# Self-attention lead-in of a four-block transformer kernel: how the second half of queries and keys, the high and low parts and the spreading transfers are ordered

## What is computed

```python
x_norm = modulate(_ln(x), shift_a, scale_a)
qkv = x_norm @ W_qkv + b_qkv
q, k, v = jnp.split(qkv, 3, axis=-1)
q = q.reshape(B, N, NH, hd).transpose(0, 2, 1, 3)    # NH = 16 heads of hd = 16, N = 1024
k = k.reshape(B, N, NH, hd).transpose(0, 2, 1, 3)
v = v.reshape(B, N, NH, hd).transpose(0, 2, 1, 3)
attn_w = jax.nn.softmax(jnp.einsum('bhqd,bhkd->bhqk', q, k) * scale, axis=-1)
attn_out = jnp.einsum('bhqk,bhkd->bqhd', attn_w, v)
```

## Time and profile before

| | |
|---|---|
| runs | 1668.72, 1672.08, 1673.46 us; median 1672.08 |
| profiled execution | 1674.23 us, its span 1672.4 us |
| busy share of the span | TensorE 91%, VectorE 63%, ScalarE 46%, GpSimd 23% |
| chain that ended last | TensorE 68%, VectorE 19%, issue 6%, ScalarE 5%, DMA 1%, GpSimd 1% |
| clock granted to TensorE | mean 0.968 of full speed |

### The profile page before, as it was taken

How to read it: one execution, slowest core, us unless ns; L and a number is a source line. 1 busy time by engine, 2 the same in 40 slices (tenths; PEclk the granted TensorE clock), 3 DMA queues, 4 the chain that set the end, 5 groups by cost and what they waited for, 6 DMA issues and landing times.

```text
span 1672.4 us, 26374 instructions
## 1 busy us (share of the span) xinstructions
PE 1528.8 (91%) x10485; PEld 927.8 (55%) x10485; DVE 1049.2 (63%) x2946; ACT 769.9 (46%) x1228; POOL 379.4 (23%) x419
## 2 busy tenths in 40 slices
PE   5899998999998999878998999899999899887898
PEld 3456574444354857556764666543444476655676
DVE  3564344999727445899457334399991744579953
ACT  1315421588853533325543533138886354333444
POOL 3510005343016000114133000344400701001320
PEclk9898999999999999999999999899999999999999
DMA  9400007221020000000130000542202000000000
GB/s 337 140 1 0 0 22 161 37 39 31 2 76 1 1 1 2 2 1 2 32 133 1 0 1 1 143 66 40 40 2 77 1 1 1 3 1 1 1 1 25
DMA packets 37551, 59.60 MB, mean 36 GB/s; under 512 B 7360, under 2 KB 26980, under 8 KB 36532
## 3 DMA queue, kind: packets, MB, share of 16 engines
q1 hardware_dynamic: 25239, 34.71, 6.3%
q0 software_dynamic: 9408, 15.85, 6.1%
q10 hardware_dynamic: 2780, 7.36, 1.2%
HBM read 42.03 MB, written 2.10 MB: 26 GB/s over the span
## 4 chain that ended last, share of the span: by engine, by line
PE 68%; DVE 19%; issue 6%; ACT 5%; DMA 1%; POOL 1%; ACTq 0%; DVEq 0%; POOLq 0%
PE ps L993 9%; PE ps L1005 8%; PE ps L464 7%; PE ps L1299 4%; PE ps L978 3%; PE ps L870 3%; PE ps L1092 3%; DVE taken L2351 3%; PE ps L1100 3%; DVE rs L2036 2%; PE ps L848 2%; PE ps L592 2%; DVE mxw L2028 2%; PE ps L600 2%; PE ps L1156 2%
## 5 line engine op out<-in xcount | busy, mean ns | idle before, releaser
L2221 DVE TENSOR_REDUCE mm<-ps 128x1 f32<-128x1024 f32 x256 | 310.2, 1223 | 32.9 <-PE ps L978 25.6
L1618 ACT ACTIVATE pt<-ps 128x512 f32<-128x512 f32 x512 | 276.8, 599 | 59.1 <-PE ps L993 41.3
L2464 POOL TENSOR_TENSOR rstd<-ve,minus_half 128x4 f32<-128x4 f32 x32 | 35.7, 1116 | 748.8 <-DVE ve L1900 748.8
L993 PE MATMUL ps<-qx,kx 64*128 64x512 f32 x512 | 188.3, 445 | 1.0 <-ACT pt L1618 1.0
L978 PE MATMUL ps<-kx,qx 48*128 48x512 f32 x512 | 186.6, 444 | 0.2
L1005 PE MATMUL ps<-pt,v 128*32 128x256 f32 x2048 | 158.7, 390 | 0.0
L993 PEld LDWEIGHTS ps<-qx,kx 64*128 64x128 f32 x512 | 78.9, 184 | 95.9 <-ACT pt L1618 85.9
L2111 DVE TENSOR_TENSOR rlo<-ring,rhi 128x512 fp32r<-128x512 f32 x48 | 33.2, 692 | 114.5 <-ACT ring L1569 114.4
L1005 PEld LDWEIGHTS ps<-pt,v 128*32 128x32 f32 x2048 | 42.9, 108 | 85.6 <-ACT pt L1618 61.7
L978 PEld LDWEIGHTS ps<-kx,qx 48*128 48x128 f32 x512 | 75.4, 184 | 22.0 <-issue 18.0
L592 PE MATMUL ps<-filler 128*128 128x512 f32 x262 | 83.6, 434 | 0.0
(11 more groups left out here) (374 smaller groups left out, 3396.1 us busy)
## 6 DMA issues: line engine op xcount, KB each, us to landing
wm<-in_L_xcond_W_mlp_dram SPq DMA_DIRECT2D x4, 1024.0 KB, 7.9
qx<-q_hi POOLq DMA_DIRECT2D x64, 64.0 KB, 2.6
kx<-k_hi POOLq DMA_DIRECT2D x64, 64.0 KB, 2.8
w3a<-in_L_xcond_w_m_dram SPq DMA_DIRECT2D x2, 2048.0 KB, 8.1
w<-in_L_xcond_e_w_dram SPq DMA_DIRECT2D x6, 512.0 KB, 7.8
w<-in_L_xcond_e_w_dram SPq DMA_DIRECT2D x2, 1536.0 KB, 13.3
s_ada<-in_L_xcond_w_ada_dram ACTq DMA_DIRECT2D x1, 2304.0 KB, 23.0
qx<-q_lo POOLq DMA_DIRECT2D x32, 64.0 KB, 2.6
```

The source lines that it names most:

```text
L993: pe.matmul(ps[:, bank, :], kx[r, p % 4, kc * P:(kc + 1) * P], qx[r, p % 4, half * 512:(half + 1) * 512], start=True, stop=True).then_inc( ...
L1618: act.activation(pt[:, u % 8, half * 512:(half + 1) * 512], ps[:, bank, :], ACT.Exp, scale=QK_SCALE).then_inc(st_read, 1)
L2221: return dve.tensor_reduce(mm[:, p % 2, e, t:t + 1], place(), X, ALU.max).then_inc(ring_read, 1)
```

## The change

The matmuls of the second half are taken out of the lead-in. Six of its eight fp32 matmuls stand one by one behind the first six units of query scores (`full_step(m + 2)`), two before the loop. The gate rows are spread behind unit 8 instead of before the loop. The nine fillers before the loop and the fillers beside units 0 to 6 go; nine fillers are put ahead of the transposes of block 1 and four behind them; the fillers beside units 7 to 15 write bank 4. The first linear of block 1 waits for each chunk of `hT` by itself. High and low parts of chunk 0 are made for 512 tokens at a time: those of block 0 ahead of ScalarE's `ln(2, 1)`, those of block 1 behind it. `full_ready` is raised for q and k separately. `spread(0)` waits for each of q high, q low, k high and k low and sends each as soon as it is there; in every spread the four high transfers of q (or k) now come before its two low ones.

The core of the diff (left out: the removed `queries_keys` and `high_parts`, and semaphore counts that only follow):

```diff
 (TensorE)
-                linear(0, wqk2, 0, hT[:, 0])
+                linear(0, wqk2, 0, hT[:, 0]).then_inc(full_done, 1)
                 residual(1, 1)
                 pe.wait_ge(v_ready, b * NB + 1)
-                linear(2, wqk2, KC, hT[:, 0])
+                linear(2, wqk2, KC, hT[:, 0]).then_inc(full_done, 1)
+                keep_busy(6, 9)
                 ln(2, 1)
+                keep_busy(6, 4)
...
+                def full_step(j):
+
+                    qk, k, c = j // 4, j // 2 % 2, j % 2
+                    if j == 4:
+                        pe.wait_ge(v_ready, b * NB + NB)
+                    ins = pe.matmul(ps[:, 4 + 2 * qk + k, :], wqk2[:, c, (qk * KC + 1) * P:(qk * KC + 2) * P], hT[:, k, c, :], start=c == 0, stop=c == KC - 1)
+                    if j == 7:
+                        ins.then_inc(full_done, 1)
...
-                pe.wait_ge(hT_ready, b * 2 * N_HT + 12)
-                for qk in range(2):
-                    queries_keys(0, qk, take(), (1,)).then_inc(ring_ready, 1)
+                linear(take() + 1, wqk2, 0, hT[:, 1], (hT_ready, b * 2 * N_HT + 10)).then_inc(ring_ready, 1)
+                linear(take() + 1, wqk2, KC, hT[:, 1]).then_inc(ring_ready, 1)
                 values(1)
-                queries_keys(1, 0, 4)
-                pe.wait_ge(v_ready, b * NB + NB)
-                queries_keys(1, 1, 6).then_inc(full_done, 1)
+                full_step(0)
+                full_step(1)
                 pe.wait_ge(v2_clear, b + 1)
-                pe.wait_ge(ring_read, b * N_RING + 2)
-                keep_busy(2, 9)
-                pe.wait_ge(full_ready, b + 1)
-                for j in range(3):
...
-                    if n < 4:
-                        keep_busy(7, 2 if n < 0 else 1)
+                    if m == 7:
+                        pe.wait_ge(full_ready, b * 2 + 1)
+                    if 7 <= m and n < 4:
+                        keep_busy(4 if m < 2 * T else 7, 2 if n < 0 else 1)
...
+                    if m < 6:
+                        full_step(m + 2)
+                    elif m == 8:
+                        pe.wait_ge(full_ready, b * 2 + 2)
+                        for j in range(3):
...
 (ScalarE)
-                ln(2, 1, (mod, M_SC_A, M_SH_A))
...
+                def high_part(qk, k):
+
+                    col = (C_BQ2, C_BK2)[qk]
+                    affine(dense[2 * qk][:, k * BLK:(k + 1) * BLK], ps[:, 2 * qk + k, :], 1.0, colT[:, col:col + 1]).then_inc(hi_ready, 1)
+
+                for qk in range(2):
+                    act.wait_ge(full_done, b * 3 + qk + 1)
+                    high_part(qk, 0)
+                ln(2, 1, (mod, M_SC_A, M_SH_A))
...
                 for qk in range(2):
-                    high_parts(0, qk)
-                act.wait_ge(full_done, b + 1)
+                    act.wait_ge(ring_ready, u0 + qk + 1)
+                    high_part(qk, 1)
+                act.wait_ge(full_done, b * 3 + 3)
...
 (VectorE)
                 for qk in range(2):
-                    low_parts(qk)
+                    low_part(qk, 0)
+                for qk in range(2):
+                    place()
+                    low_part(qk, 1).then_inc(ring_read, 1)
                 add_v2(1)
...
 (GpSimd)
-                    if p == 0:
-                        pool.wait_ge(ring_read, b * N_RING + 2)
...
                     for qk, wide in enumerate((qx, kx)):
-                        for e in range(2):
-                            r = 32 * (p % 4) + HD * e
-                            for i, part in enumerate(((0, 1, 0), (0, 0, 1))[qk]):
-                                pool.dma_start(wide[64 * e + HD * i:64 * e + HD * (i + 1), p % 4, :], dense[2 * qk + part][r:r + HD, :]).then_inc(spread_ld[p % 4], 16)
+                        for part in range(2):
+                            if p == 0:
+                                if part == 0:
+                                    pool.wait_ge(hi_ready, b * 6 + 2 + qk + 1)
+                                else:
+                                    pool.wait_ge(ring_read, b * N_RING + qk + 1)
+                                pool.sem_inc(passed, 1)
+                            for e in range(2):
+                                r = 32 * (p % 4) + HD * e
+                                for i in range(3):
+                                    if ((0, 1, 0), (0, 0, 1))[qk][i] == part:
+                                        pool.dma_start(wide[64 * e + HD * i:64 * e + HD * (i + 1), p % 4, :], dense[2 * qk + part][r:r + HD, :]).then_inc(spread_ld[p % 4], 16)
```

More of the change, by code:

```diff
@@ L963, in take_key @@
                     return 4 + n % 3
-                def queries_keys(c, qk, bank, blocks=range(NB)):
-                    for k in blocks:
-                        ins = linear(bank + k, wqk2, qk * KC + c, hT[:, k])
-                    return ins
+                def full_step(j):
[5 more added lines that the diff above has]
+                        ins.then_inc(full_done, 1)
                 def query_scores(p, u):
@@ L1049, in _ @@
                         query_scores(q, at_m)
+                    if m < 6:
[3 more added lines that the diff above has]
+                        for j in range(3):
+                            o = N_ROW * b + R_G_A + j
+                            ins = pe.matmul(ps[:, 5 + j // 2, j % 2 * D:(j % 2 + 1) * D], row_of[:, o:o + 1].broadcast_to([64, P]), row_hl[:, :], start=True, stop=True)
+                        ins.then_inc(gates_spread, 1)
                     if n >= 0:
@@ L1626, in _ @@
                 for qk in range(2):
-                    high_parts(0, qk)
-                act.wait_ge(full_done, b + 1)
+                    act.wait_ge(ring_ready, u0 + qk + 1)
+                    high_part(qk, 1)
+                act.wait_ge(full_done, b * 3 + 3)
                 for qk in range(2):
                     col = (C_BQ2, C_BK2)[qk] + 1
-                    ins = affine(full[qk], ps[:, 4 + 2 * qk:6 + 2 * qk, :].rearrange("p a q -> p (a q)"), 1.0, colT[:, col:col + 1])
-                ins.then_inc(full_ready, 1)
+                    affine(full[qk], ps[:, 4 + 2 * qk:6 + 2 * qk, :].rearrange("p a q -> p (a q)"), 1.0, colT[:, col:col + 1]).then_inc(full_ready, 1)
                 act.wait_ge(gates_spread, b + 1)
@@ L1635, in _ @@
                 act.activation(gates[:, 2, :], ps[:, 6, 0:D], ACT.Copy).then_inc(gates_ready, 1)
-                act.wait_ge(full_ready, b + 1)
+                act.wait_ge(full_ready, b * 2 + 2)
                 for i in range(4):
@@ L1639, in _ @@
                 for qk in range(2):
-                    high_parts(1, qk)
+                    act.activation(dense[2 * qk][:, :], full[qk], ACT.Copy).then_inc(hi_ready, 1)
                 scored = 2
@@ L2211, in place, with low_part @@
                     return ps[:, 2 * (n % 2):2 * (n % 2) + 2, :].rearrange("p a q -> p (a q)")
[L2213 to L2217 removed]
+                def low_part(qk, k):
+                    dve.wait_ge(hi_ready, b * 6 + 2 * k + qk + 1)
+                    col, r = (C_BQ2, C_BK2)[qk], slice(k * BLK, (k + 1) * BLK)
+                    return dve.scalar_tensor_tensor(dense[2 * qk + 1][:, r], ps[:, 2 * qk + k, :], colT[:, col:col + 1], dense[2 * qk][:, r].bitcast(F32),
+                                                    ALU.add, ALU.subtract)
                 def query_maximum(p, u):
```

18 lines of the change are left out of this document (1 added, 17 removed).

## The result

The changed kernel takes 1716.12 us in the median of four runs (1713.93 to 1719.25), the kernel before 1672.12: the ratio is 1.0255, with a 95% interval of 1.0236 to 1.0275. It is 44 us slower where 12 us faster was forecast. The profiled execution took 1716.97 us, 42.7 more than that of before.

What follows compares the result with a forecast made beforehand. TensorE's chain and waits up to unit 0 were taken as the bound: 6.4 and 7.4 us gained in the batches, 13.8, less 1.8 for the clock, gives 12.0 and 1660.1 us; range 1655.5 to 1667.5.

Steps and rivals of the forecast that it cites:

- Fillers round the transposes: Around block 1's transposes: fillers keep the clock at 2.4 GHz, so k's linear ends 3.2 us earlier.
- Halves: Block 1's high parts made 512 columns at a time, 0.60 us each: q ready at 262.3, k at 264.1.
- piece by piece: Spread 0 on GpSimd: issues start at 262.95, after q's high part; all landed at 271.5 instead of 278.3.
- landings: Spread 0's transfers land 2.5 to 3.2 us after issue; 3.15 us taken.
- Rival C: Transfers come later because VectorE's work holds up GpSimd's issues: gains of only 5 to 9 us, 1663 to 1667; chance 0.13.
- The new wait ahead of unit 0: TensorE, after two full steps, has nothing to do for 2.9 us until the transfers land at 271.5.
- the sum of 13.8: Gain of both batches without any clock effect: 6.4 us in the first, 7.4 us in the second.
- The clock at unit 0: The new wait may drop the clock under units 0 to 5: 1.7 to 3.5 us lost, chance six in ten a batch.
- Rival E: Clock falls at unit 0 and stays low through the lead: 14.5 us more a batch, 15 us slower, 1687; chance 0.03.
- the lead lost: Units before unit 9 get denser with full steps: 2.4 us lost a batch, 3.1 if changes of shape cost extra.
- a limit of 1.223 us a unit: VectorE's reduction time for each unit of query scores; nine need 11.0 us, so it isn't the lead's bound.
- The cover of 0.35 us for ScalarE's copy of the maxima: Before the key scores: GpSimd's spreads move 6.75 us earlier, TensorE 6.4, so the copy is not late.

Runs made afterwards that it cites:

- e1_cover: The changed kernel with eleven fillers in the wait ahead of unit 0, also called the covered kernel: 1662.45 us median, ratio 0.9929.
- the burst: The changed kernel with 24 fillers in one go ahead of unit 7: 1690.03 us median, ratio 1.0078.
- the four fillers: The changed kernel with four fillers instead of two beside units 7 to 21: 1744.5 and 1719.18 us.

## Why the prediction was wrong

**What was right.** The parts up to unit 0. Fillers round the transposes keep the clock (3.70 us for the linears; without them 5.21, worth 4.8 us in the two batches). Halves and piece by piece bring the transfers forward (2.7 and 2.5 us for the four waits). Unit 0 comes 9.1 and 10.3 us sooner where 8.8 and 9.8 were forecast; landings took at most 2.8 us instead of the 3.15 I took. Rival C did not come: from the first to the last issue of spread 0 it was 5.5 us, 5.4 before, with VectorE's low parts beside it. The new wait ahead of unit 0 was named and sized: 2.9 us forecast, 2.57 and 2.35 measured. With the clock held (`e1_cover`), unit 9 starts 6.2 and 7.1 us sooner against the linear of k's block 0, 6.4 and 7.4 forecast, so the sum of 13.8 stands at 13.3.

The Trainium skill, DMA: Bandwidth & Descriptors, section Anatomy of one DMA, has the fit behind the estimate of 2.15 us a landing: this case's trace is nearer to it than to my 3.15, with 2.2 at the least and 2.5 in the middle.

**The step that failed** is "The clock at unit 0". It said that the wait is nearly the one after which the clock fell, gave it six chances in ten a batch, and then priced the fall at 1.7 to 3.5 us, "after unit 0 there is none, so 3 to 7 us". It lasted 68 us and cost 28.6 us a batch. The price was taken from the low stretches of the earlier trace rows, and those ended under the linears, matmuls of 128 rows with nothing between them. I carried their length over to a stretch of quite different work, assuming that a busy TensorE gets its clock back. The burst and the four fillers show that it doesn't under score matmuls of 48 rows and fillers in turn. The same mix holds a clock that is already high, so the trace of before could not show it in the lead: there the clock was at 1.00 when the lead began. A warning stood elsewhere in that trace, though, where small matmuls of several shapes follow each other with one pause of 1.5 us among them. The clock is low for 17 us there, over twice the 7 us that I took as the most (columns as in rows 3):

```profile
118.50:134.50 16.00, 14.50 (x42) 0.50 0.01 1
```

Rival E, that the clock stays down through the lead, was the mechanism to the letter. It had a chance of 0.03 and 14.5 us a batch. Its argument against, "no pause in the lead", is what the runs refute. Its price was wrong as well, by its own sum: 29 us is what the 22 units take at the full clock, and half a us for each us at half clock holds only for us spent there. From unit 0 to the first key scores it was 54.0 us, against 31.3 with the clock held: 22.7 us more, not 14.5. The other 6 us came behind the lead, where the low clock went on for 15 us. A lesson lay in the code: the nine fillers of the kernel before stood just where the wait was (without them alone it is 1707 and 1724 us). I priced their removal as time freed and as cover lost for one short stretch, not as what the whole lead rested on.

**Smaller misses.** Units with a full step are 1.72 us apart, not 1.54, so the lead lost 2.9 us, near the 3.1 given as the upper bound for changes of shape. VectorE isn't a limit of 1.223 us a unit in the lead: with one filler, units came 1.09 us apart at first. The price of rival C was a misreading: the 0.64 us of the earlier trace rows is the length of one record, and the issues of spread 3 start 0.48 us apart, as those of spread 0 do. The cover of 0.35 us for ScalarE's copy of the maxima did hold in the covered kernel and failed by 0.53 us where the lead was made shorter, with a fall of the clock behind it.

**Open.** Why an equal wait tips the clock in one batch and not in the next; why a kernel with no wait ahead of unit 0 (14 fillers) falls at unit 8; and what in the lead keeps the low clock low, and in the first values ends it.

## What to carry to other kernels

Before fillers are taken out, or a TensorE wait is opened, look at what runs behind it: price a fall of the clock by how long the following work keeps it low, not by the low stretches found elsewhere in the trace. Here score matmuls of 48 rows in turn with others mostly held a high clock and did not win it back in up to 85 us; where such a stretch follows, cover the waits ahead of it, with work that is anyway due where there is some. A cover is no guarantee: the kernels with one still had runs with a lower mean clock. And when a kernel's times spread in steps far larger than its noise, read the mean clock of each run, and the granted clock of each batch, before explaining the median.

## What was not expected of the hardware

The high and the low clock are both steady under one and the same instruction stream: 28.5 us of the lead at 1.00 in the first batch and 68 us at 0.50 in the second, in one execution of the kernel before without its nine fillers. Waits of 0.53 us (unit 22) and 0.55 us (unit 7) were followed by a fall, while 0.55 us at the same unit 7 in the covered kernel was not. But for the burst, the low clock ended 3.1 to 7.6 us behind the first weighted values, eleven times of eleven, with TensorE busy before and after. Eleven matmuls that compute nothing, 3.08 us in all, are worth 54 us (1716.12 against 1662.45).
